# Four-layer token model on one core: semaphore clears in mid-stage, a key cache filled during the projection before attention, attention's first mask and values first

## The chip, the cores and the metric

The kernel runs on one core of a Trainium2 chip, as one launch. A core has five engines with a queue each: TensorE (PE, with PEld for its weight loads), VectorE (DVE), ScalarE (ACT), GpSimd (POOL) and SyncE (SP), which issues nearly all DMAs here. The metric is the device time of one execution in microseconds (us); before the change the median of three runs is 3574.46 us (3572.65 to 3577.14).

## The reference, cut to what matters

2048 tokens of width 512 pass through four layers, each a conditional product and a feed-forward part added to the tokens. The layer around the change is the third: attention with grouped heads over a paged cache of keys and values.

```
q = einsum(x, Wq)  [32 heads x 128];  k, v = einsum(x, Wk), einsum(x, Wv)  [8 heads x 128]
q, k = rope(rmsnorm(q)), rope(rmsnorm(k))
kc, vc = k_cache[block_table], v_cache[block_table]       # 16 pages of 32 tokens for each sequence
k_all, v_all = concat([kc, k]), concat([vc, v])           # 512 cached + 32 new tokens
scores = einsum(q, k_all) * SCALE;  scores where cached token >= cache_seqlens: -1e30
o = softmax(scores) @ v_all;   x = x + lora_mix(o @ Wo)
```

All of it is float32. Each product is made as three TensorE passes over a high and a low part of both operands: ScalarE copies the tile rounded (the high part, fp32r), and VectorE or GpSimd subtracts that from the tile (the low part).

## The kernel before, in words

The program is a row of stages, each one function and one block of code for the five engines: `l0_cond`, `l0_ffn`, `l1_up`, `l1_down`, `moe` (kind 1, which gives x2), `l2_qkv`, `l2_attn`, `l2_out`, `moe` (kind 2), `l3`. A stage takes its semaphores and on-chip memory when it begins and gives the memory back when it ends. All engines meet at the end of each block (a DRAIN of each queue, then an exchange of semaphores), so no engine starts the next stage before the slowest has ended this one. The order inside a queue is the order of the code; nothing plans it at run time.

Semaphores of a stage are cleared by SP in the stage after it, by `before.clear(sp)`, one instruction for each semaphore (line 54). In eight of the nine stages that have it this is SP's last work before the block ends; in `l3` it stands between the last store and the waits for the last eight stores to land.

In `l0_ffn` SP does for each of the 16 token tiles: fetch a later x tile, wait until VectorE has finished this tile (`done`), store it (line 500), load four numbers from a table and issue four small DMAs for `wg` (line 504).

`l2_qkv` keeps the tokens, turned (`xT`, 64 KB in each partition for both parts), and runs 8 head groups x 16 token tiles = 128 steps: 24 matmuls for q, k, v; ScalarE copies and squares (1722, 1725, 1729), VectorE sums and applies the cosine, GpSimd the sine and the root (1673, 1676), ScalarE scales (1695), PE turns the heads (1807), ScalarE and VectorE split them in parts (1702, 1706, 199), SP stores them (1626, 1629, 1649). Slots for the stored tiles are two deep: ScalarE waits until the store two steps back has landed. One DMA at the start of the eighth head group already fetches the first 16 pages of the key cache into `stage`.

`l2_attn` has 2 halves of heads x 64 sequences = 128 groups of 4 units. `Kall` holds the 64 pages of a half's key cache as high and low parts. It is made in four chunks of 16 pages: fetch into one of three stage buffers (1 MB), high part on ScalarE (line 2017), low part on VectorE or GpSimd (line 199). Then, for each group, VectorE and GpSimd copy the 16 pages that the sequence's table names from `Kall` into `K` (line 1901), two buffers deep. VectorE adds the new keys (2059) and makes the mask (2063). A unit is: scores on PE (line 194), add mask and take the maximum on VectorE (2092), exponential on ScalarE (2041), scaling on VectorE (2102, 2105), and five and six units later the turning of the probabilities (2156) and the product with the values (2170, 2171). GpSimd gathers the values (1997). Before its loop VectorE makes the row numbers of the values (2069), converts the lengths (2071), makes the low parts of chunks 0, 2 and 3, copies 10 pages of the first group and makes its mask; GpSimd makes the low part of chunk 1 and copies 6 pages. Chunks 4 to 7 belong to the second half of the heads.

Of the kernel before, what the change touches and what calls it, by code (L numbers as in the profile page):

```python
# [6 lines left out]
F32 = mybir.dt.float32  # L7
# [6 lines left out]
P = 128  # L14
NT = 16
# [7 lines left out]
class Stage:  # L23
# [22 lines left out]
    def slots(self, name, n, shape, dt=F32, each=1, sems=None):  # L46
        return Slots(self, name, n, shape, dt, each, sems)
# [9 lines left out]
class Slots:  # L57
# [3 lines left out]
    def __init__(self, st, name, n, shape, dt, each, sems):  # L61
        self.n, self.each = n, each
        self.bufs = [st.sb(f"{name}{i}", shape, dt) for i in range(n)]
        self.sems = sems or [st.sem(f"{name}{i}") for i in range(n)]
# [347 lines left out]
def l0_ffn(nc, A, S, before):  # L412
# [62 lines left out]
    with nc.Block() as block:  # L475
        @block.sync
        def _(sp):
# [28 lines left out]
            before.clear(sp)  # L506
# [170 lines left out]
def l1_up(nc, A, S, before):  # L677
# [62 lines left out]
    with nc.Block() as block:  # L740
        @block.sync
        def _(sp):
# [45 lines left out]
            before.clear(sp)  # L788
# [160 lines left out]
def l1_down(nc, A, S, before):  # L949
# [39 lines left out]
    with nc.Block() as block:  # L989
        @block.sync  # L990
        def _(sp):
# [45 lines left out]
            before.clear(sp)  # L1037
# [276 lines left out]
def moe(nc, A, S, before, kind, Beside):  # L1314
# [5 lines left out]
    base = st.pair("base", [P, 4, D])  # L1320
    gc = st.pair("gc", [P, 4, G + P])
    bt = st.pair("bt", [P, 1, D])
    dT = [st.pair(f"dT{i}", [P, 4, P]) for i in range(8)]
# [24 lines left out]
    with nc.Block() as block:  # L1348
        @block.sync
        def _(sp):  # L1350
# [34 lines left out]
            before.clear(sp)  # L1385
# [186 lines left out]
def l2_qkv(nc, A, S, before):  # L1572
    st = Stage(nc, "l2q")
    ident, _ = S["ident"]
    xT = st.pair("xT", [P, 4, 2048])
    wq = [st.pair(f"w{i}", [P, 4, 768]) for i in range(2)]
    w = Weights(st, 3, 768, [(*sl(wq[hg % 2], S_, slice(k, k + 1), S_), rows_of(A["wqkv"][hg], k, 1)) for hg in range(8) for k in range(4)])
    pa = [st.ps(f"pa{i}", [P, 1024]) for i in range(2)]
# [20 lines left out]
    N = len(steps)  # L1599
    begin, finish = {0: 0, 1: 1, 6: 2, 8: 3}, {5: 0, 7: 1, 10: 2, 12: 3}  # L1600
# [12 lines left out]
    with nc.Block() as block:  # L1613
        @block.sync
        def _(sp):
# [15 lines left out]

            for k in range(3):
                w.fetch(sp, k)
            for k in range(10, 16):
                sp.wait_ge(*before_x.landed(k))
# [5 lines left out]
            for n, (hg, tt) in enumerate(steps):  # L1641
                if n == 7 * NT:
                    sp.dma_start(st0[:, :, :], A["kT"][0, 0:16].rearrange("a p n -> p a n")).then_inc(st0_in, 16)
# [6 lines left out]
                if n >= 2:  # L1650
                    stores(n - 2)
            stores(N - 2)
            stores(N - 1)
            before.clear(sp)

        @block.gpsimd
        def _(pool):
            pool.memset(half[:, :], -0.5).then_inc(half_set, 1)
# [20 lines left out]
        def _(act):  # L1679
# [32 lines left out]
            for n, (hg, tt) in enumerate(steps):  # L1712
# [19 lines left out]
                if n >= 2:  # L1732
                    turned_parts(n - 2)
# [842 lines left out]
```

## Time and profile before

| | us |
|---|---|
| median of 3 runs | 3574.46 |
| the profiled execution | 3580.38 |
| its span, first to last instruction | 3578.6 |
| busy PE, DVE, ACT, POOL | 3332.9, 2323.6, 1762.9, 1386.7 |

A group of instructions is named by line, engine, operation, output and inputs. "Idle before" is time in which the engine stood still just before the instruction, with what ended the wait. The stages end, in us from the span's start, at 96.7, 405.6, 784.6, 965.1, 1083.8, 1724.3, 3020.9, 3383.4 and 3489.1, and the last at 3578.6.

### The profile page before, as it was taken

How to read it: one execution, taken by the hardware profiler on the slowest of the kernel's cores; microseconds unless marked ns; L12 is line 12 of the kernel's file. 1: busy time of each engine (PE TensorE's matmuls, PEld its weight loads, DVE VectorE, ACT ScalarE, POOL GpSimd, SP SyncE). 2: the span in 40 equal slices, each digit the busy share in tenths (PEclk: the TensorE clock that was granted, in tenths of full speed). 3: DMA queues.
4: the chain of work that ended last, by engine and by line, in shares of the span. 5: the costliest groups of instructions: out<-in, count | busy, mean ns of one | idle time of the engine just before them, and what ended most of it. 6: DMA issues, size and time to landing. Idle time of an engine off the chain costs nothing. (4 is left out here: it accounts for less than half of the span.)

```text
span 3578.6 us, 69531 instructions
## 1 busy us (share of the span) xinstructions
PE 3332.9 (93%) x22314; PEld 3076.0 (86%) x22314; DVE 2323.6 (65%) x6558; ACT 1762.9 (49%) x4289; POOL 1386.7 (39%) x2439
## 2 busy tenths in 40 slices
PE   7899699989788999999499999989999998999888
PEld 5688699988677888888499999989999998888677
DVE  5444343334286877777688988878888886422274
ACT  3322122223225777887466666656666665322222
POOL 0221100000035777887455655645565563100022
PEclk9899799999889999999799999999999999999999
DMA  5310442324335555555666666656666665533333
GB/s 202 127 55 25 96 110 81 81 90 146 92 114 162 168 175 178 172 180 164 202 210 212 220 209 211 221 171 212 220 209 212 219 211 188 180 109 109 109 115 121
DMA packets 444290, 562.49 MB, mean 157 GB/s; under 512 B 170712, under 2 KB 330264, under 8 KB 427033
## 3 DMA queue, kind: packets, MB, share of 16 engines
q1 hardware_dynamic: 424216, 419.63, 37.9%
q0 software_dynamic: 19712, 138.42, 11.2%
q8 instruction: 180, 2.95, 0.3%
q14 instruction: 182, 1.48, 0.1%
HBM read 389.36 MB, written 168.56 MB: 156 GB/s over the span
## 5 line engine op out<-in xcount | busy, mean ns | idle before, releaser
L1901 POOL CAST l2a_K<-l2a_Kall 128x256 fp32r x1524 | 597.4, 442 | 428.1 <-issue 422.2
L194 PE MATMUL l2a_s<-l2a_K,l2a_Q 128*128 128x288 f32 (+1 forms) x3072 | 521.1, 306 | 49.0 <-DVE l2a_K L2059 38.6
L2170 PE MATMUL l2a_x<-l2a_pt,l2a_V 128*128 128x128 f32 x4096 | 543.0, 276 | 4.9 <-DVE l2a_pn L2111 4.9
L2170 PEld LDWEIGHTS l2a_x<-l2a_pt,l2a_V 128*128 128x128 f32 x4096 | 503.9, 193 | 5.4 <-issue 5.2
L194 PEld LDWEIGHTS l2a_s<-l2a_K,l2a_Q 128*128 128x128 f32 x3072 | 428.3, 192 | 50.2 <-issue 49.3
L2092 DVE CUSTOM_DVE_ANT_0 l2a_sm<-l2a_s,l2a_B 128x544 f32<-128x544 f32 x512 | 369.3, 721 | 92.0 <-PE l2a_s L194 80.1
L2041 ACT ACTIVATE l2a_p<-l2a_sm,l2a_st 128x544 f32<-128x544 f32 x512 | 379.6, 741 | 31.1 <-DVE l2a_st L2095 29.8
L2027 ACT ACTIVATE l2a_pt<-l2a_t 128x512 f32<-128x512 f32 x512 | 305.6, 597 | 127.8 <-PE l2a_t L2156 127.1
L142 POOL TENSOR_TENSOR moe_btL<-moe_stage,moe_btH 128x512 fp32r<-128x512 f32 x2 | 5.7, 2850 | 881.5 <-ACT moe_btH L137 881.5
L2156 PE MATMUL l2a_t<-ident,l2a_p 128*128 128x128 f32 x2048 | 335.4, 286 | 5.9 <-ACT l2a_ao L2034 5.9
L2156 PEld LDWEIGHTS l2a_t<-ident,l2a_p 128*128 128x128 f32 x2048 | 287.9, 209 | 7.2 <-issue 6.6
L2102 DVE TENSOR_SCALAR l2a_p<-l2a_p,l2a_st 128x512 f32<-128x512 f32 x512 | 281.6, 550 | 18.2
L2034 ACT ACTIVATE l2a_ao<-l2a_x 128x128 f32<-128x128 f32 x512 | 142.2, 278 | 281.8 <-PE l2a_x L2171 281.8
L1673 POOL TENSOR_TENSOR l2q_rot<-l2q_qs,sinq 128x256 f32<-128x256 f32 x256 | 192.1, 772 | 137.2 <-ACT l2q_qs L1722 137.2
L1695 ACT ACTIVATE l2q_qn<-l2q_qn,l2q_r 128x128 f32<-128x128 f32 x640 | 200.3, 396 | 0.8 <-DVE l2q_qn L1778 0.8
L2171 PE MATMUL l2a_x<-l2a_pn,l2a_vn 128*128 128x128 f32 x1024 | 198.5, 276 | 0.0
L1676 POOL TENSOR_TENSOR l2q_r<-l2q_r,l2q_eps 128x5 f32<-128x5 f32 x128 | 193.4, 1511 | 0.0
L1769 DVE TENSOR_REDUCE l2q_r<-l2q_sq 128x5 f32<-128x640 f32 x128 | 105.2, 822 | 117.1 <-ACT l2q_sq L1729 117.0
L194 PE MATMUL l2q_pa<-l2q_w0H,l2q_xTH 128*128 128x512 f32 (+1 forms) x512 | 178.8, 349 | 0.0
L194 PE MATMUL l2q_pa<-l2q_w1H,l2q_xTH 128*128 128x512 f32 (+1 forms) x512 | 178.1, 348 | 0.0
L194 PE MATMUL l2q_pa<-l2q_w0H,l2q_xTL 128*128 128x512 f32 (+1 forms) x512 | 173.6, 339 | 0.0
L194 PE MATMUL l2q_pa<-l2q_w1H,l2q_xTL 128*128 128x512 f32 (+1 forms) x512 | 172.9, 338 | 0.0
(812 smaller groups left out, 8856.1 us busy)
## 6 DMA issues: line engine op xcount, KB each, us to landing
s_qT<-l2q_qo SPq DMA_DIRECT2D x128, 512.0 KB, 3.0
l2a_Q<-s_qT SPq DMA_DIRECT2D x128, 512.0 KB, 5.9
s_ao<-l2a_ao SPq DMA_DIRECT2D x64, 512.0 KB, 5.0
l2o_a<-s_ao SPq DMA_DIRECT2D x128, 256.0 KB, 3.1
s_kn<-l2q_ko SPq DMA_DIRECT2D x128, 128.0 KB, 3.1
l2a_kn<-s_kn SPq DMA_DIRECT2D x32, 512.0 KB, 5.8
l2q_stage<-in_wqkv SPq DMA_DIRECT2D x32, 384.0 KB, 4.1
s_act<-l1u_ac SPq DMA_DIRECT2D x88, 128.0 KB, 1.9
```

The costliest lines, as they stand in the source:

```text
L194: i = pe.matmul(out, a, b, start=start and m + z == 0, stop=stop and 3 * m + z == n - 1)
L1673: pool.tensor_tensor(r[:, hs, a], q[:, hs, z], sn[:, tt, a].unsqueeze(1).broadcast_to([P, hs.stop - hs.start, 64]), ALU.mult).then_inc(tur ...
L1676: pool.tensor_tensor(f[:, 10:15], f[:, 5:10], half[:, :], ALU.pow).then_inc(rooted, 1)
L1695: act.activation(o[:, h, :], o[:, h, :], ACT.Copy, scale=f[:, 10 + h:11 + h]).then_inc(scaled, 1)
L1901: e.tensor_copy(K[:, j:j + 1, :, :].rearrange("p a z n -> p a (z n)"), Kall[:, bass.ds(v, 1), :, :].rearrange("p a z n -> p a (z n)")).the ...
L2027: act.activation(ptr[tr % 2][:, :, :], ps_t[tr % 2][:, :, :], ACT.Copy).then_inc(t_copied, 1)
L2041: act.activation(prr[sc % 6][:, :], smr[sc % 2][:, :], ACT.Exp, bias=s[:, 1:2], scale=SCALE, accum_out=s[:, 2:3]).then_inc(exped, 1)
L2092: dve.tensor_tensor_reduce(out=smr[sc % 2][:, :], in0=ps_s[sc % 2][:, 224:768], in1=Br[g % 2][:, :], scale=1.0, scalar=-3e38, op0=ALU.add, ...
L2102: dve.tensor_scalar(p[:, 0:512], p[:, 0:512], s[:, 3:4], None, ALU.mult).then_inc(scaled, 1)
L2156: m = pe.transpose(ps_t[tr % 2][:, k, :], p[:, k:512:4], ident[:, :])
L2170: pe.matmul(px[:, P:256], V[:, k * D + hg * P:k * D + hg * P + P], pt[:, k, :], start=k == 0, stop=False)
L2171: pe.matmul(px[:, P:256], vn[:, hg, :], pnr[g % 2][:, :], start=False, stop=True).then_inc(pv_mm, 1)
```

## The change

1. `before.clear(sp)` moves from the end of the stage into its middle: after the middle tile (`l0_ffn`, both `moe`), after the fourth of eight column groups (`l1_up`), after the third of four (`l1_down`), after half the head groups, units or steps (`l2_qkv`, `l2_attn`, `l2_out`), and after tile 11 of 16 in `l3`. In `l0_ffn` the table load and the four `wg` DMAs of a tile go ahead of the wait for `done` and the store.
2. Memory for the key cache (`cache`, 64 KB in each partition), the first group's keys (`keys`) and `head` is taken before `moe` kind 1. The tiles of `moe` kind 1 lie in `cache`, and then `xT` of `l2_qkv` does, one slice for each token tile. The weights of the even head groups lie in `keys` and `head`.
3. In the sixth head group of `l2_qkv` SP fetches, one in each step, the 16 pages of the first sequence by its table. In the eighth, each step has one more high part (ScalarE) and low part (VectorE) of four pages: steps 0 to 3 make the first sequence's keys straight into `keys`, steps 4 to 15 make cache pages 0 to 47 in the places of the token tiles that are no longer needed. SP also fetches the first group's q and new keys, and leaves pages 48 to 63 fetched but not split. GpSimd waits at the start of `l2_qkv` for the last stores of x2.
4. `l2_attn` starts with that. VectorE: new keys, lengths, mask of group 0, then the row numbers of the values; chunk 3's low part comes after the first unit's maximum. GpSimd gathers the first group's values first and then copies 12 pages for the second. Chunks 4, 5 and 6 are fetched in units 4, 8 and 12.

```diff
@@ l0_ffn, SP
                 x_tile(tt + 2)
-                sp.wait_ge(done, tt + 1)
-                sp.dma_start(S["x1"][tt * P:(tt + 1) * P, :], xr[tt][:, :]).then_inc(xr.sem(tt), 16)
                 sp.reg_load(r, subj[0:1, 4 * tt:4 * tt + 4])
                 for j in range(4):
...
+                sp.wait_ge(done, tt + 1)
+                sp.dma_start(S["x1"][tt * P:(tt + 1) * P, :], xr[tt][:, :]).then_inc(xr.sem(tt), 16)
+                if tt == NT // 2:
+                    before.clear(sp)
-            before.clear(sp)
@@ l2_qkv, SP
+            def cache_pages(i):
+                sp.wait_ge(part_lo, i - 3)
+                sp.dma_start(st0[:, 4 * (i % 4):4 * (i % 4) + 4, :],
+                             A["kT"][0, 4 * (i - 4):4 * (i - 3)].rearrange("a p n -> p a n")).then_inc(st0_in[i % 4], 16)
...
+                if hg == 5:
+                    page(tt)
+                if hg == 7 and tt >= 1:
+                    cache_pages(tt + 3)
+                if n == 7 * NT + 1:
...
+                    sp.dma_start(q0..., S["qT"][0, 0]).then_inc(q0_in, 16)
+                    sp.dma_start(kn0..., S["kn"][0, 0]).then_inc(kn0_in, 16)
+                if n == 4 * NT:
+                    before.clear(sp)
             stores(N - 2)
+            cache_pages(19)
             stores(N - 1)
-            before.clear(sp)
@@ l2_qkv, ScalarE and VectorE, at the end of a step
+                if hg == 7:
+                    act.wait_ge(*key_part_in(tt))
...
+                    act.activation(key_part(tt, 0), st0[:, 4 * (tt % 4):4 * (tt % 4) + 4, :], ACT.Copy).then_inc(part_hi, 1)
+                if hg == 7:
+                    dve.wait_ge(part_hi, tt + 1)
+                    low_part(dve, [key_part(tt, z) for z in range(2)], st0[:, 4 * (tt % 4):4 * (tt % 4) + 4, :]).then_inc(part_lo, 1)
@@ l2_attn, GpSimd
             pool.wait_ge(rows_set, 2)
+            values(0)
             pool.wait_ge(tab_in, 16)
-            low(1)
-            for n in range(4):
-                chunk_done(pool, n)
-            page_copies(pool, r, 0, range(10, 16), pages_g)
+            chunk_done(pool, 3)
@@ l2_attn, ScalarE
-            for n in range(4):
-                high(n)
+            high(3)
@@ l2_attn, VectorE
-            for n in (0, 2, 3):
-                low(n)
-            for n in range(4):
-                chunk_done(dve, n)
-            page_copies(dve, r, 0, range(5), pages_v)
-            page_copies(dve, r, 0, range(5, 10), pages_v)
+            new_keys(0)
...
             mask(0)
...
+                    if sc == 0:
+                        low(3)
+                        chunk_done(dve, 3)
+                        dve.wait_ge(tab_in, 16)
```

## Rows read from the trace of the kernel before

**Rows 1.** The page: busy time, share of the span, instructions of an engine.

```profile
PE 3332.9 (93%) x22314; PEld 3076.0 (86%) x22314; DVE 2323.6 (65%) x6558; ACT 1762.9 (49%) x4289; POOL 1386.7 (39%) x2439
```

**Rows 2.** Busy time by stretch: us, engines, granted clock, DMA share, GB/s.

```profile
1640.00:1715.00 75.00, 72.51 (x446) 64.77 (x445) 56.79 (x113) 57.62 (x160) 56.51 (x81) 1.00 0.52 169
1724.30:1757.30 33.00, 0.00 (x0) 0.00 (x0) 12.82 (x18) 7.64 (x4) 8.83 (x12) 0.50 0.73 208
```

**Rows 3.** Line 54 by stretch, six of nine: ns min/median/max, first to last start.

```profile
L54 SPq EVENT_SEMAPHORE_RANGE_CLEAR  x39: 25/25/49, 402.8 to 405.4; - x39
L54 SPq EVENT_SEMAPHORE_RANGE_CLEAR  x41: 25/25/29, 782.2 to 784.4; - x41
L54 SPq EVENT_SEMAPHORE_RANGE_CLEAR  x30: 25/25/25, 1082.0 to 1083.6; - x30
L54 SPq EVENT_SEMAPHORE_RANGE_CLEAR  x43: 25/25/34, 1721.7 to 1724.1; - x43
L54 SPq EVENT_SEMAPHORE_RANGE_CLEAR  x23: 25/25/40, 3487.2 to 3488.8; - x23
L54 SPq EVENT_SEMAPHORE_RANGE_CLEAR  x36: 25/25/25, 3576.0 to 3577.9; - x36
```

**Rows 4.** Timeline of SP around the end of l0_ffn: start, us, instruction.

```profile
400.06 0.35 SPq L500 DMA_DIRECT2D s_x<-l0f_xr  x1
400.91 1.83 SPq L504 DMA_DIRECT2D wg<-in_w  x4
```

**Rows 5.** Line 475, l0_ffn's block end: GpSimd's drain, in ns.

```profile
L475 POOLq DRAIN  x1: 2693/2693/2693, 398.0 to 398.0; - x1
```

**Rows 6.** Lines 1034 and 2218, the stores of d, and their time to landing.

```profile
L1034 SPq DMA_DIRECT2D s_d<-l1d_o x16: 319/320/532, 844.9 to 962.2; - x16
DMA to landing us min/median/max: 2.3/2.4/3.6
L2218 SPq DMA_DIRECT2D s_d<-l2o_o x16: 319/320/338, 3118.2 to 3380.8; - x16
DMA to landing us min/median/max: 2.4/2.8/4.5
```

**Rows 7.** Timeline of SP: first loads that read the stage before.

```profile
966.18 0.93 SPq L1355 DMA_DIRECT2D moe_dr<-s_d  x2
...
3022.50 1.29 SPq L2203 DMA_DIRECT2D l2o_a<-s_ao  x3
...
3384.72 0.93 SPq L1355 DMA_DIRECT2D moe_dr<-s_d  x2
```

**Rows 8.** Timeline of the start of attention.

```profile
1726.97 0.41 DVE L2069 TENSOR_SCALAR l2a_rows<-l2a_tabx,l2a_pr 128x64 int32<-128x64 int32 x2 [6.03 <-DMA l2a_pr<-in_p]
...
1734.50 4.51 POOL L199 TENSOR_TENSOR l2a_Kall<-l2a_stage,l2a_Kall 128x2048 fp32r<-128x2048 f32 x1 [9.15 <-ACT l2a_Kall L2017]
...
1736.90 2.15 DVE L2071 CAST l2a_seq<-l2a_seqi 128x64 f32<-128x64 int32 x1 [9.52 <-DMA l2a_seqi<-in_seq]
...
1749.74 2.29 DVE L199 TENSOR_TENSOR l2a_Kall<-stage,l2a_Kall 128x2048 fp32r<-128x2048 f32 x1 [6.29 <-ACT l2a_Kall L2017]
...
1753.96 6.82 POOL L1901 CAST l2a_K<-l2a_Kall 128x256 fp32r x18 [14.96 <-issue]
...
1757.35 5.62 PE L194 MATMUL l2a_s<-l2a_K,l2a_Q 128*128 128x288 f32 x24 [38.58 <-DVE l2a_K L2059]
...
1759.09 0.72 DVE L2092 CUSTOM_DVE_ANT_0 l2a_sm<-l2a_s,l2a_B 128x544 f32<-128x544 f32 x1 [1.33 <-PE l2a_s L194]
...
1767.51 0.71 DVE L2092 CUSTOM_DVE_ANT_0 l2a_sm<-l2a_s,l2a_B 128x544 f32<-128x544 f32 x1
```

**Rows 9.** Timeline of one steady step of l2_qkv.

```profile
1645.11 0.71 ACT L1722 ACTIVATE l2q_qs<-l2q_pa 128x640 f32<-128x640 f32 x1 [1.14 <-PE l2q_pa L194]
...
1645.89 1.45 POOL L1673 TENSOR_TENSOR l2q_rot<-l2q_qs,sinq 128x256 f32<-128x256 f32 x2 [1.17 <-ACT l2q_qs L1722]
...
1646.64 0.82 DVE L1769 TENSOR_REDUCE l2q_r<-l2q_sq 128x5 f32<-128x640 f32 x1 [1.08 <-ACT l2q_sq L1729]
```

More of the change, by code:

```diff
@@ L1036, in _ @@
                     fetch(cb + 2, range(FT))
-            before.clear(sp)
+                if cb == 2:
+                    before.clear(sp)
         @block.scalar
@@ L1319, in moe, with pair @@
     ident, _ = S["ident"]
[L1320 to L1323, printed above, removed]
+    pair = st.pair
+    if kind == 1:
+        room = S["cache"][:, :, :, :].rearrange("p a z n -> p (a z n)")
+        taken = [0]
+        def pair(name, shape):
+            n = int(np.prod(shape[1:]))
+            at, taken[0] = taken[0], taken[0] + 2 * n
+            return tuple(room[:, at + z * n:at + z * n + n].rearrange("p (a n) -> p a n", a=shape[1]) for z in range(2))
+    base = pair("base", [P, 4, D])
+    gc = pair("gc", [P, 4, G + P])
+    bt = pair("bt", [P, 1, D])
+    dT = [pair(f"dT{i}", [P, 4, P]) for i in range(8)]
     dr = st.slots("dr", 6, [P, 4, P])
@@ L1651, in _ @@
                     stores(n - 2)
+                if n == 4 * NT:
+                    before.clear(sp)
             stores(N - 2)
+            cache_pages(19)
             stores(N - 1)
-            before.clear(sp)
         @block.gpsimd
         def _(pool):
+            for k in range(10, 16):
+                pool.wait_ge(*before_x.landed(k))
             pool.memset(half[:, :], -0.5).then_inc(half_set, 1)
@@ L1829, in l2_qkv @@
     before.marks.close()
-    S["qkv_stores"] = [(r, N - 2 + i) for r in (qo, ko, vs) for i in range(2)]
+    S["qkv_stores"] = qo, ko, vs
     return st
@@ L1841, in l2_attn @@
     st0, st0_in = S["stage"]
-    stage = [(st0, st0_in)] + [st.const(f"stage{i}", [P, 16, P]) for i in range(2)]
-    Kall = st.sb("Kall", [P, NB, 2, P], F32R)
+    stage = [(st0, st.sem("stage0"))] + [st.const(f"stage{i}", [P, 16, P]) for i in (1, 2)]
+    Kall, K0, (q0, q0_in), (kn0, kn0_in) = S["cache"], S["keys"], S["q0"], S["kn0"]
     tab, tab_in = st.const("tab", [1, NB * 16], I32)
@@ L2080, in _ @@
             mask(0)
+            dve.wait_ge(tabx_in, 16)
+            dve.wait_ge(pr_in, 16)
+            for h in range(2):
+                dve.tensor_scalar(rows[:, h, :], tabx[:, :], 8.0, pr[:, h:h + 1], ALU.mult, ALU.add).then_inc(rows_set, 1)
             for i in range(U + LV):
@@ L2491, in build @@
         stage = ExitStack()
-        S["stage"] = stage.enter_context(nc.sbuf_tensor("stage", [P, 16, P], F32)), outer.enter_context(nc.semaphore("s_stage"))
+        S["stage"] = (stage.enter_context(nc.sbuf_tensor("stage", [P, 16, P], F32)),
+                      [outer.enter_context(nc.semaphore(f"s_stage{i}")) for i in range(4)])
+        S["cache"] = stage.enter_context(nc.sbuf_tensor("cache", [P, NB, 2, P], F32R))
+        S["keys"] = stage.enter_context(nc.sbuf_tensor("keys", [P, 17, 2, P], F32R))
+        S["head"] = stage.enter_context(nc.sbuf_tensor("head", [P, 3072], F32R))
+        for i, n in enumerate(("q0", "kn0")):
+            S[n] = (S["head"][:, 1024 * i:1024 * i + 1024].rearrange("p (h z x) -> p h z x", h=4, z=2),
+                    outer.enter_context(nc.semaphore(f"s_{n}")))
         with ExitStack() as mid:
```

141 lines of the change are left out of this document (86 added, 55 removed).

## The prediction

> **What bounds the kernel now.** I read the engines' busy time first: PE is busy 93% of the span and the others far less [rows 1]. So time goes either with PE's own work, which this change leaves alone, or with the stretches where PE stands. The table by stretch shows both: in the projection (`l2_qkv`) PE is busy 72.5 of 75 us at the full granted clock, while for the 33 us at the start of attention it has no matmul at all [rows 2]. That gap is the largest target. The timeline of its start says what is late: VectorE and GpSimd split four chunks of the key cache and copy the first group's pages, and PE's first scores at 1757.35 end 38.58 us of idleness [rows 8]. The rows of line 54 show the second target: at the end of each stage SP clears 23 to 43 semaphores one after the other, while every other engine stands at the block's end [rows 3]. Six of the nine runs stand there; the three others (ends of `l1_down`, `l2_attn`, `l2_out`) look alike.
>
> **Part 1, the clears.** What counts is when the block would end without them, and whether the next stage then finds its data. In mid-stage they cost nothing, I say: SP has waits in each stage, and its next issues come a few us ahead of need. If that cover were gone, each run of clears would cost at most its own 1.6 to 2.6 us once.
>
> - `l0_ffn`: the last x1 store is issued at 400.06 + 0.35; after it come 4 `wg` DMAs (1.83) and the clears up to 405.4 [rows 3, 4]. With the DMAs ahead of the wait, both go. GpSimd's drain ends at 398.0 + 2.7 = 400.7, and that becomes the last [rows 5]. 405.4 - 400.7 = 4.7 us.
> - `l1_up`: 782.2 to 784.4 and the last one's own time: 2.3 us [rows 3]. The next stage begins with weights and tiles stored long before.
> - First `moe` to `l2_qkv`: 1082.0 to 1083.6 is 1.7 us [rows 3]. The first weights are fetched that much earlier. One more small DMA (the table) stands before the token loads, 0.3 us at the issue; the weights' chain is the longer, so I keep 1.7. GpSimd's new wait for x2 holds up a memset and one low part whose weight has not landed yet: nothing.
> - `l2_qkv` to `l2_attn`: 1721.7 to 1724.1, 2.4 us [rows 3].
> - Second `moe` to `l3`: 3487.2 to 3488.8, 1.7 us [rows 3]; `l3` begins with weights.
> - `l1_down` to `moe`: here the next stage must read what was just stored. The last store starts at 962.2 and lands 2.4 later at the median, so at 964.6 [rows 6]; the first load of d could be issued at about 964.8 instead of 966.18 [rows 7]. 1.4 us, between 0.4 (its longest landing, 3.6) and 2.3 (the clears whole).
> - `l2_out` to `moe`: 3380.8 + 2.8 = 3383.6 [rows 6] against 3384.72 [rows 7]: 1.0 us, between 0 and 2.1.
> - `l2_attn` to `l2_out`: the first load of the attention output goes at 3022.50 [rows 7], nearly 2 us into the stage, and before it stand only one weight fetch and the wait for the last store. It will go then again. Only the weights are ahead of it: 0.4 us, between 0 and 1.4.
> - End of `l3`: the last clear starts at 3577.9 [rows 3] and stands beside the landing of the last store, which takes 2 us like the others in [rows 6]: 0.3 us, between 0 and 0.5.
>
> Sum: 4.7 + 2.3 + 1.7 + 2.4 + 1.7 + 1.4 + 1.0 + 0.4 + 0.3 = 15.9 us.
>
> **Part 2, the start of attention.** I compare the moment of unit 4's maximum, the first of the second group, from which both kernels run alike. It is 1767.51 now, 8.4 us after unit 0's at 1759.09 [rows 8]. With the clears gone the stage starts at about 1722.0 (1721.7 and the exchange at the block's end) [rows 3]. Then:
>
> - Data for the mask: nothing large is queued ahead now. Of DMAs in attention's first microseconds, the row numbers' inputs were there at 1726.97, 2.6 us into the stage [rows 8]; the new order puts the lengths and `iota` (272 KB) first, behind the last stores and the last 256 KB of key pages. I take 3.5 us: 1725.5. Bounds: 2.6, and 8 us (the lengths came 12.6 us after the stage's start with 3 MB around them, at 1736.90 [rows 8], so I take under that).
> - VectorE: new keys are done by then; conversion 0.2, mask 0.7 (as wide as the 0.72 of a maximum), row numbers 0.41. Unit 0's maximum at 1726.8. PE has its scores long before.
> - After it VectorE has one thing more than now, chunk 3's low part, 2.29 [rows 8]. ScalarE's high part (no longer than that, begun with the stage or when the last pages land) is ready. Unit 4 at 1726.8 + 8.4 + 2.3 + 0.1 = 1737.6.
> - GpSimd must not be later: low part done at 1730.1, then 12 page copies at 6.82 / 18 = 0.38 each [rows 8], 4.6 us: 1734.7. Unit 4's scores are due at about 1736. It fits with 1.3 us.
>
> Gain 1767.5 - 1737.6 = 29.9 us, of which 2.4 is the clears' already: 27.5 us here. Bounds 21 and 29.5.
>
> A row shows a conversion of 128x64 taking 2.15 us on VectorE (1736.90) while GpSimd's low part runs from 1734.50 for 4.51; both end at 1739.0 [rows 8]. I price it at 0.2 because in the new order GpSimd has only its memsets (about 1 us) then. The Trainium skill (SBUF — State Buffer, section "SBUF: two separate sides") says that VectorE and GpSimd share a pair of ports under an exclusive lock which the loser waits for during the whole instruction. The row agrees. By this rule the same lock speaks against part 3: the added low part there has two inputs on chip.
>
> **Part 3, what the eighth head group now carries.** 16 steps each get a high part of 128x512 on ScalarE and a low part on VectorE, 0.6 us (0.71 for 128x640 [rows 9]) and 0.7 us (a quarter of the chunk's 2.29 [rows 8] and a fixed part). A step takes about 4.7 us (446 matmuls, 29 a step, in 72.5 us [rows 2]), and both engines have room in it: ScalarE waits 1.14 us for PE, VectorE 1.08 for ScalarE [rows 9]. The low part comes right before that wait, so 0.4 us of room is left on each. On SP each step gains one DMA, 0.7 us at most, behind a wait for the low part of the step before; queued behind it is the store of v and then those of q and k, whose slots ScalarE needs two steps or 9.4 us later; with some 3 us to land (2.4 to 2.8 for such stores [rows 6]) and 2 us to fill and split, I estimate 4 us to spare. DMA traffic rises from 169 GB/s at a share of 0.52 [rows 2] by 256 KB per step, 55 GB/s, to a share of about 0.69. Nothing shows on PE: 0 us, between 0 and 10 (0.6 us a step, the whole high part, if the room is not where I see it). Pages and first group's q: single DMAs beside the same steps, nothing. If the rule of the shared ports holds, GpSimd begins its products (1645.89 [rows 9]) up to 0.35 us late in each step; it stands idle 1.17 us before them, so the rule would cost nothing until VectorE's part moves by 0.8 us, and then at most 0.35 x 16 = 5.6 us, which lies inside those bounds.
>
> **Part 4, small debts.** Chunks 4, 5 and 6 were fetched while PE stood and now fall on units 4, 8 and 12, 1 MB each beside q and values: 0.5 us, between 0 and 5. PE's granted clock was 0.50 over the 33 us [rows 2]; the new start has sparse scores for 15 us, so PE may still be at 1.2 GHz when the work gets dense: 1 us, between -1 and 4. `xT` and the tiles of `moe` kind 1 in other memory: the same shapes and runs, 0.
>
> **The sum.** 15.9 + 27.5 - 0.5 - 1.0 = 41.9 us. Against the profiled execution: 3580.38 - 41.9 = 3538.5. The median is 5.9 us lower than that execution: 3574.46 - 41.9 = 3532.5.
>
> **Rivals.**
>
> - *The projection pays.* For: the room on ScalarE and VectorE is only about 1.1 us, and the new work takes 0.6 to 0.7 of each and ties SP, ScalarE and VectorE in one more ring. Against: PE fills the step and waits for none of them. Price: 1 us a step, 16 us: 3548.5. Chance 0.08.
> - *The first unit waits for its DMAs.* Lengths and `iota` land 8 us into the stage instead of 3.5, behind the last stores: 4.5 us less, 3537. For: they were very late before. Against: those 3 MB are no longer there. Chance 0.12, together with a later chunk 3.
> - *Only the clears pay.* The second group's keys become what all waits for: chunk 3's fetch must land in full, go through ScalarE and VectorE, and then through 12 copies on GpSimd, and this chain replaces the old one. Price, were the start of attention to save nothing beyond the waits at its ends: 3574.5 - 15.9 = 3558.6. Against: three of four chunks are split before. Chance 0.02.
> - *Slower.* The place is the eighth head group's stores: SP's wait for the low part delays the stores of q and k, their slots come free late, ScalarE stops, the low part gets later still. It decides at 41.9 / 16 = 2.6 us a step, 7.3 instead of 4.7; at 3.2 us a step the time is 3574.5 + 9.5 = 3584. Against: it needs stores some 4 us later than they are. Chance 0.03.
> - *The moves do less harm than I price*, and loads after a block's end find their data at once: 3528. Chance 0.05.
>
> **How the numbers follow.** 0.70 is left for the forecast, with its own range 3528 to 3537. For 8 in 10 the range reaches up over the DMA rival and into the projection's and down over the last: 3525 to 3544. About 0.2% (7 us) is what a measurement of this kernel tells from no change: above 3567 only the slower rival and slips that I did not see: faster 0.95, same 0.02, slower 0.03.
>
> **What would show it.** Line 54 in the middle of each stage and SP's first issue of a stage within 0.3 us of its last one before, 4.7 us earlier against `l0_ffn`'s last store. PE's first scores within 1 us of the start of attention; unit 0's maximum 5 us and unit 4's 15.6 us after it. Steps of the eighth head group still 4.7 us apart, with ScalarE's and VectorE's waits shrunk to about half a microsecond. I am wrong if those steps grow, if unit 4 waits for GpSimd's copies, or if a long wait for values appears in the first four groups.

## The result, and the profile after

The changed kernel takes 3534.98 us at the median of four runs (3528.07 to 3536.73); the kernel before, with them, 3575.8 (3572.65 to 3579.39). The ratio, estimated from all runs, is 0.9882 (95% interval 0.9865 to 0.9899), and the medians differ by 40.8 us where 41.9 were forecast. A second series (kernel 4 below) gave 3533.99 against 3575.59, 0.9881 (0.9866 to 0.9896), 41.6 us.

The two profiled executions differ by more, 3580.38 - 3528.07 = 52.3 us, because this one of the changed kernel was its fastest and that of the kernel before was slower than all four of its timed runs. The stages' lengths, read between the ends of their blocks, show where (us; mean granted clock in brackets where it moved):

| stage | before | after | difference |
|---|---|---|---|
| `l0_ffn` | 308.9 (0.89) | 295.3 (0.92) | -13.6 |
| `l1_up` | 379.0 | 373.7 | -5.3 |
| `l1_down` | 180.5 | 176.6 | -3.9 |
| first `moe` | 118.7 | 115.8 | -2.9 |
| `l2_qkv` | 640.5 | 639.5 | -1.0 |
| `l2_attn` | 1296.6 | 1270.4 | -26.2 |
| `l2_out` | 362.5 | 362.3 | -0.2 |
| second `moe` | 105.7 | 104.0 | -1.7 |
| `l3` | 89.4 (0.92) | 92.0 (0.89) | +2.6 |

Busy time on the page, against [rows 1]: every engine has nearly the same work as before, so what went is mostly idle time, and in `l0_ffn` some of PE's busy time, by its clock.

```profile
PE 3330.7 (94%) x22314; PEld 3073.8 (87%) x22314; DVE 2323.7 (66%) x6562; ACT 1767.3 (50%) x4302; POOL 1384.0 (39%) x2432
```

The table by stretch of the changed kernel (us, then the busy time of PE, PE's weight loads, VectorE, ScalarE and GpSimd with instructions, granted clock, DMA share, GB/s): `l0_ffn`, the eighth head group, and the start of attention up to the second group's first scores. The last two answer to [rows 2].

```profile
96.70:391.80 295.10, 272.38 (x1264) 228.08 (x1264) 127.53 (x232) 76.41 (x124) 73.93 (x69) 0.92 0.20 65
...
1610.00:1686.00 76.00, 76.00 (x467) 67.84 (x466) 67.19 (x127) 65.48 (x175) 61.18 (x81) 1.00 0.69 214
1697.40:1714.40 17.00, 6.59 (x25) 5.77 (x25) 10.52 (x28) 4.45 (x7) 7.59 (x16) 0.50 0.64 199
```

The eighth head group carries the new parts at the full clock, with PE busy in all of its 76 us and at the DMA share of 0.69 that was forecast. The 33 us without a matmul have become 17 with 25 of them. `l0_ffn` before had 281.63 us of PE at a clock of 0.89: 9.25 us of the 13.6 are the same 1264 matmuls run at a higher granted clock.

Line 54 of the changed kernel, three of nine stages, against [rows 3]: the same counts, in mid-stage, 12 us (`l3`) and more before its end.

```profile
L54 SPq EVENT_SEMAPHORE_RANGE_CLEAR  x39: 25/25/34, 307.0 to 309.1; - x39
```
```profile
L54 SPq EVENT_SEMAPHORE_RANGE_CLEAR  x43: 25/25/31, 1393.5 to 1396.2; - x43
```
```profile
L54 SPq EVENT_SEMAPHORE_RANGE_CLEAR  x36: 25/25/40, 3511.4 to 3513.7; - x36
```

SP's timeline around the end of `l0_ffn` (start, us, instruction), against [rows 4], and GpSimd's drain against [rows 5]:

```profile
391.06 0.35 SPq L506 DMA_DIRECT2D s_x<-l0f_xr  x1
391.94 0.35 SPq L159 DMA_DIRECT2D l1u_nat<-s_x  x1
```
```profile
L476 POOLq DRAIN  x1: 2693/2693/2693, 389.0 to 389.0; - x1
```

From the start of the last store to that of the next stage's first issue it is 0.88 us now. The drain ends at 389.0 + 2.69 = 391.7, the stage at 391.8.

SP's stores of d and the first loads of it (ns min/median/max, first to last start; then start and us), against [rows 6, 7]:

```profile
L1037 SPq DMA_DIRECT2D s_d<-l1d_o x16: 319/320/516, 824.5 to 941.5; - x16
```
```profile
L2292 SPq DMA_DIRECT2D s_d<-l2o_o x16: 319/320/333, 3067.0 to 3329.6; - x16
```
```profile
944.24 0.93 SPq L1369 DMA_DIRECT2D moe_dr<-s_d  x2
...
2971.32 0.81 SPq L2277 DMA_DIRECT2D l2o_a<-s_ao  x2
...
3332.78 0.38 SPq L1369 DMA_DIRECT2D moe_dr<-s_d  x1
```

The timeline of the start of attention, against [rows 8]; the stage begins at 1697.5:

```profile
1697.59 0.35 SPq L2013 DMA_DIRECT2D l2a_iota<-in_iota  x1
1697.98 1.05 SPq L2014 DMA_DIRECT2D l2a_seqi<-in_seq  x1
1698.41 3.06 PE L195 MATMUL l2a_s<-keys,head 128*128 128x288 f32 x12 [4.18 <-DVE keys L2130]
1703.51 0.20 DVE L2143 CAST l2a_seq<-l2a_seqi 128x64 f32<-128x64 int32 x1 [5.24 <-DMA l2a_seqi<-in_seq]
1703.81 0.50 DVE L2139 TENSOR_SCALAR l2a_B<-l2a_iota,l2a_seq 128x544 f32<-128x544 f32 x1
1704.55 0.72 DVE L2162 CUSTOM_DVE_ANT_0 l2a_sm<-l2a_s,l2a_B 128x544 f32<-128x544 f32 x1
1705.38 2.28 DVE L200 TENSOR_TENSOR cache<-stage,cache 128x2048 fp32r<-128x2048 f32 x1
1708.99 5.13 POOL L1971 CAST l2a_K<-cache 128x256 fp32r x12 [3.02 <-issue]
1714.32 3.06 PE L195 MATMUL l2a_s<-l2a_K,l2a_Q 128*128 128x288 f32 x12 [3.01 <-POOL l2a_K L1971]
1716.06 0.72 DVE L2162 CUSTOM_DVE_ANT_0 l2a_sm<-l2a_s,l2a_B 128x544 f32<-128x544 f32 x1 [0.34 <-PE l2a_s L195]
```

PE's first scores come 0.9 us into the stage instead of 33. VectorE then waits for the lengths until 1703.51, 6.0 us in. Unit 0's maximum is at 7.0 and unit 4's at 18.6; before they were at 34.8 and 43.2. PE's second group waits 3.01 us, for GpSimd's copies.

The last step of the eighth head group, against [rows 9]:

```profile
1686.52 0.70 ACT L1782 ACTIVATE l2q_qs<-l2q_pa 128x640 f32<-128x640 f32 x1 [0.62 <-PE l2q_pa L195]
1686.98 0.68 DVE L200 TENSOR_TENSOR cache<-stage,cache 128x512 fp32r<-128x512 f32 x1
1687.31 1.63 POOL L1733 TENSOR_TENSOR l2q_rot<-l2q_qs,sinq 128x256 f32<-128x256 f32 x2 [0.87 <-ACT l2q_qs L1782]
1688.05 0.82 DVE L1836 TENSOR_REDUCE l2q_r<-l2q_sq 128x5 f32<-128x640 f32 x1 [0.39 <-ACT l2q_sq L1789]
1690.00 0.63 ACT L1800 ACTIVATE cache<-stage 128x512 fp32r<-128x512 f32 x1
```

The parts cost 0.63 and 0.68 us; ScalarE's wait fell from 1.14 to 0.62, VectorE's from 1.08 to 0.39, GpSimd's from 1.17 to 0.87, and its two products took 1.63 instead of 1.45. Over the first 14 steps of that head group the mean waits of ScalarE and VectorE are 0.66 and 0.45 us, against 1.13 and 1.07 before.

One thing in `l2_qkv` did change outside this head group. VectorE's sum of squares runs once in each of the 128 steps; its row before and after (last two figures: first and last start):

```profile
L1769 DVE TENSOR_REDUCE l2q_r<-l2q_sq x128: 821/822/825, 1103.8 to 1712.9; 128x5 f32<-128x640 f32 x128
```
```profile
L1836 DVE TENSOR_REDUCE l2q_r<-l2q_sq x128: 821/822/824, 1077.6 to 1688.1; 128x5 f32<-128x640 f32 x128
```

The same 127 steps take 609.1 us before and 610.5 after. It is in every head group from the second on: its 16 steps take 75.76 us in each of the four profiles with the tiles in their old places (before, kernels 1, 2 and 9), and 75.95 or 76.05 in each of the ten with the new ones (kernel 6's eighth group aside). That is 0.19 or 0.29 us for each of seven head groups, 1.3 to 2.0 us in the stage. (The two profiles of the changed kernel itself, this one and kernel 4's, have 75.95 and 76.05.)

### The profile page after: what moved, and what is told of

Same layout as the page of the kernel before. It is cut to its first block and busy times, and to the rows that moved or that the text cites. A ratio compares the mean times of both kernels' runs of the same rounds, so it can differ in the third digit from the quotient of the medians.

```text
span 3526.3 us, 69602 instructions
## 1 busy us (share of the span) xinstructions
PE 3330.7 (94%) x22314; PEld 3073.8 (87%) x22314; DVE 2323.7 (66%) x6562; ACT 1767.3 (50%) x4302; POOL 1384.0 (39%) x2432
## 5 line engine op out<-in xcount | busy, mean ns | idle before, releaser
L1971 POOL CAST l2a_K<-cache 128x256 fp32r x768 | 295.3, 434 | 222.4 <-issue 222.4
L1971 POOL CAST keys<-cache 128x256 fp32r x750 | 299.2, 449 | 187.8 <-issue 149.9
L195 PE MATMUL l2a_s<-keys,head 128*128 128x288 f32 (+1 forms) x1536 | 262.2, 307 | 17.8 <-POOL l2a_K L1971 7.2
L195 PE MATMUL l2q_pa<-keys,cache 128*128 128x512 f32 (+1 forms) x1024 | 268.4, 344 | 0.0
L195 PE MATMUL l2q_pa<-l2q_w1H,cache 128*128 128x512 f32 (+1 forms) x1024 | 267.7, 344 | 0.0
L195 PE MATMUL l2a_s<-l2a_K,l2a_Q 128*128 128x288 f32 (+1 forms) x1536 | 261.0, 306 | 3.4 <-POOL l2a_K L1971 3.0
L195 PEld LDWEIGHTS l2a_s<-keys,head 128*128 128x128 f32 x1536 | 215.0, 193 | 18.9 <-issue 16.1
L195 PEld LDWEIGHTS l2a_s<-l2a_K,l2a_Q 128*128 128x128 f32 x1536 | 214.5, 192 | 3.9 <-issue 3.3
L195 PEld LDWEIGHTS l2q_pa<-keys,cache 128*128 128x128 f32 x1024 | 180.9, 190 | 21.7
L195 PEld LDWEIGHTS l2q_pa<-l2q_w1H,cache 128*128 128x128 f32 x1024 | 180.2, 189 | 21.6
```

The source lines that it names most:

```text
L195: i = pe.matmul(out, a, b, start=start and m + z == 0, stop=stop and 3 * m + z == n - 1)
L1971: e.tensor_copy(K[:, j:j + 1, :, :].rearrange("p a z n -> p a (z n)"), Kall[:, bass.ds(v, 1), :, :].rearrange("p a z n -> p a (z n)")).the ...
```

## The experiments

Each is compared with runs of the kernel before on the same chip. Kernels 1 to 4 shared a chip, 5 to 8 another, 9 to 12 a third, with 12 in a series of its own; across series the ratios are compared, and 0.001 is 3.6 us. A gain is the difference of two medians and can lie 1 to 1.5 us from what the ratio gives. Lengths of stages are those of one profiled execution.

### 1 to 4. The two halves apart

1: the kernel before with the clears in mid-stage. 2: this, and `l0_ffn`'s DMAs ahead of the wait. 3: the changed kernel with the clears at the ends and the old order in `l0_ffn`. 4: the changed kernel again.

```diff
@@ 1, from the kernel before: the form for l0_ffn and moe; in the other stages the condition names their own middle
+                if tt == NT // 2:
+                    before.clear(sp)
-            before.clear(sp)
```

> The kernel before with only the semaphore clears moved to mid-stage; the order of the wg DMAs in l0_ffn and all of the key cache as before. My theory: each stage end loses its run of clears where the next stage does not wait for a landing: 13.8 us less than before (15.9 of the prediction less 2.1 for the wg DMAs), 12 to 16. Rival (the changed kernel's profile shows l0_ffn 13.8 us shorter and l1_up 5.3, so the clears in mid-stage did more than vanish from the end): 22 us or more. Rival (mid-stage clears hold up SP's DMAs and cost elsewhere): under 8 us.

> As e1_clears, and in l0_ffn the table load and the four wg DMAs of a tile ahead of the wait for done and the store. My theory: 15.9 us less than before, 2.1 less than e1_clears. Rival (the order of these DMAs, not the clears, makes l0_ffn 13.8 us shorter): 8 us or more less than e1_clears.

> The changed kernel with the clears back at the end of each stage and the old order in l0_ffn: the key cache, first mask and values alone. My theory: 26 us less than before (27.5 less 1.5 of small debts); the changed kernel's profile has unit 4's maximum 18.5 us into attention against 43.2, so 24.7 us if the projection pays nothing. Rival (the eighth head group pays 1 us a step): 9 us. With e2_clears_order it should add up to the whole: 41.

> The changed kernel again, beside the others on one chip: 41 us less than before (39 to 44), the sum of e2_clears_order and e3_keys_only within 2 us. Rival (the parts share a gain, or one spoils another): the sum is off by over 3 us. If the 52 us between the two profiled executions are the change's and not a matter of the granted clock in l0_ffn, its stage is shorter than 297 us in this profile too and its granted clock 0.92 against 0.89.

| | median | before | ratio (95%) | gain |
|---|---|---|---|---|
| 1 clears | 3562.83 | 3575.59 | 0.9967 (0.9953-0.998) | 12.8 |
| 2 clears and order | 3555.97 | 3575.59 | 0.9949 (0.9936-0.9963) | 19.6 |
| 3 the rest alone | 3553.01 | 3575.59 | 0.9934 (0.9921-0.9948) | 22.6 |
| 4 all | 3533.99 | 3575.59 | 0.9881 (0.9866-0.9896) | 41.6 |

The halves add up: 19.6 + 22.6 = 42.2 against 41.6. Both pay, in the sizes forecast within some 4 us: 15.9 for kernel 2's part, and 27.5 - 0.5 - 1.0 = 26.0 for kernel 3's; both figures lie inside the intervals. That the clears alone pay (3558.6) is thereby refuted as the whole story: it is half of it. Kernel 2 is 6.9 us below kernel 1 where 2.1 were expected, nearer to its rival (8 or more, from the order of `l0_ffn`'s DMAs); kernel 9 tests that. In kernel 4's profile `l0_ffn` took 298.6 us at a granted clock of 0.91, so the 295.3 at 0.92 above is not the changed kernel's steady figure.

### 5. The mask's inputs fetched in `l2_qkv`

```diff
@@ l2_qkv, SP, n == 7 * NT + 1; these tiles now lie in the two token buffers
+    for n_, src_ in (("iota", A["iota544"]), ("seqi", row_bc(A["seq"], NB)),
+                     ("tabx", A["tabx"]), ("pr", A["p8"])):
+        sp.dma_start(S["e_" + n_][0], src_).then_inc(S["e_" + n_][1], 16)
@@ l2_attn, SP: these four DMAs go; VectorE, after new_keys(0):
+            for r_ in S["qkv_stores"]:
+                for k_ in range(8 * NT - 2, 8 * NT):
+                    dve.wait_ge(*r_.landed(k_))
```

> The changed kernel with iota, lengths and the inputs of the row numbers fetched in the eighth head group of the projection (into the two token buffers, free by then) instead of at the start of attention; VectorE waits for the projection's last stores before the mask, since its tiles lie where these stores read. In the changed kernel the first unit's maximum stands at 7.0 us into attention, after a wait for the lengths that ends at 6.0. My theory (DMA landing after the block's end is the term I undersized, 6.0 us against 3.5): unit 0 at 3.5 to 4.5 us, unit 4 at 15 to 16 instead of 18.5, 3 us less than the changed kernel. Rival (GpSimd's 12 page copies for the second group set unit 4): the first units come early, unit 4 moves by under 1 us, same time.

3530.17 us against 3576.13, 0.9874 (0.9857 to 0.9892): 46.0 us. In attention the step is clear: 1266.8 us against 1270.4 in the changed kernel and 1270.2 in kernel 4. Its start, at 1703.2, on the timeline:

```profile
1704.05 3.06 PE L195 MATMUL l2a_s<-keys,head 128*128 128x288 f32 x12 [4.21 <-DVE keys L2128]
...
1706.24 0.20 DVE L2144 CAST l2a_seq<-nat 128x64 f32<-128x64 int32 x1 [2.34 <-DMA s_kn<-l2q_ko]
...
1707.29 0.72 DVE L2163 CUSTOM_DVE_ANT_0 l2a_sm<-l2a_s,l2a_B 128x544 f32<-128x544 f32 x1
...
1711.72 5.10 POOL L1973 CAST l2a_K<-cache 128x256 fp32r x12 [3.02 <-issue]
...
1717.04 3.06 PE L195 MATMUL l2a_s<-l2a_K,l2a_Q 128*128 128x288 f32 x12 [2.99 <-POOL l2a_K L1973]
```

Unit 0's maximum is 4.1 us into the stage instead of 7.0, unit 4's 15.6 instead of 18.6. The wait that is left, 2.34 us, is for the last stores. Attention took 1269.7 to 1270.4 us in the five other profiles whose clears and chunks stand as in the changed kernel (4, 6, 8, 10, 12), so 3.5 us is well outside what this stage varies by. So the lengths' DMA held the whole start, and all that follows moved by what it lost. The total, 0.0007 under kernel 4's ratio, goes the same way but does not show it by itself. PE's wait for GpSimd's copies stayed at 3 us: that chain begins with chunk 3's low part, behind the first maximum.

### 6. The parts of the eighth head group twice

ScalarE makes each high part a second time and VectorE each low part.

```diff
+                    act.wait_ge(part_hi, 2 * tt + 1)
+                    act.activation(key_part(tt, 0), st0[...], ACT.Copy).then_inc(part_hi, 1)
...
+                    dve.wait_ge(part_lo, 2 * tt + 1)
+                    low_part(dve, [key_part(tt, z) for z in range(2)], st0[...]).then_inc(part_lo, 1)
```

> The changed kernel with the high and the low part of each of the 16 steps of the eighth head group made twice (the same values). This uses up the room that the prediction claims: 0.6 us more on ScalarE and 0.7 us more on VectorE in each step, of some 0.6 and 0.4 left. My theory: PE's steps grow, but by no more than what goes over the room, 0.2 to 0.5 us a step, 3 to 8 us in all. Rival (the two engines are as good as full now, each part is paid whole): 10 us or more. Other rival (PE never waits for them at all, two steps of slack): under 1 us.

3544.81 against 3576.13, 0.9906 (0.9889 to 0.9922), so 0.0025 or 9 us above kernel 4's ratio; `l2_qkv` took 648.5 us against 639.5 and 640.2. A stretch of that head group, and three instructions from its timeline:

```profile
1632.00:1708.00 76.00, 70.85 (x427) 61.75 (x425) 74.51 (x131) 70.51 (x178) 63.83 (x73) 1.00 0.64 200
```
```profile
1660.57 1.58 ACT L1755 ACTIVATE l2q_qn<-l2q_qn,l2q_r 128x128 f32<-128x128 f32 x5 [0.45 <-DVE l2q_qn L1847]
...
1661.23 1.94 DVE L200 TENSOR_TENSOR cache<-stage,cache 128x512 fp32r<-128x512 f32 x2
1661.86 1.50 POOL L1733 TENSOR_TENSOR l2q_rot<-l2q_qs,sink 128x64 f32<-128x64 f32 x2
```

VectorE is busy 74.51 of 76 us and ScalarE now waits for it, not for PE; a step takes 5.25 us (from VectorE's pair at 1655.98 to the next at 1661.23) instead of 4.75. So the room that hid the change's parts was there and was nearly used up: of a second pair of parts, 8 to 9 us came through, at or just over the top of the 3 to 8 expected and under the 10 of the rival. VectorE is the engine that would have become the bound.

### 7. Chunks 4, 5 and 6 at the front

The first three fetches of 1 MB go ahead of the units again, as before the change, with the second group's q ahead of them.

```diff
+            fetch(1)
+            for n in (4, 5, 6):
+                start_chunk(n)
             for i in range(U + LV):
...
-                    if sc in (4, 8, 12):
-                        start_chunk(sc // 4 + 3)
```

> The changed kernel with key chunks 4, 5 and 6 (1 MB each) fetched right at the start of attention, after the second group's q, as the kernel before did, instead of in units 4, 8 and 12. My theory: in units 4 to 12 they cost almost nothing (0.5 us), so at the front they can only cost: 0 to 5 us more, where the first values land later. Rival (they disturb values and q in the first groups): 2 us or more less.

3536.62, 0.9881 (0.9861 to 0.9901): no difference in total. Attention took 1272.7 us, 2.3 to 2.5 more than with them moved. Its timeline shows the bill, 23 us into the stage (which began at 1707.7):

```profile
1711.82 5.45 SPq L1991 DMA_DIRECT2D l2a_stage<-in_kT  x2
...
1722.88 5.06 SPq L2010 DMA_DIRECT2D l2a_vn<-s_vn  x4
...
1730.85 1.93 PE L2245 MATMUL l2a_x<-l2a_pt,l2a_V 128*128 128x128 f32 x8 [1.81 <-DMA l2a_vn<-s_vn]
...
1734.58 0.72 DVE L2163 CUSTOM_DVE_ANT_0 l2a_sm<-l2a_s,l2a_B 128x544 f32<-128x544 f32 x1 [2.07 <-PE l2a_s L195]
```

PE waits for new values queued behind the chunks, and unit 7's maximum waits 2.07 us for PE. Spreading the fetches saves these 2 us; in units 4, 8 and 12 they cost nothing I could find.

### 8, 10 and 12. Why `l3` got longer

`l3` took 92.0 us instead of 89.4. The difference is there after its first four steps, at a lower granted clock, though its own clears only come later. 8: the second `moe`'s clears at its end again. 10: `l3`'s. 12: both.

```diff
@@ 8 and 12, moe
-                if tt == NT // 2:
+                if tt == (NT // 2 if kind == 1 else NT - 1):
@@ 10 and 12, l3
-                if tt == NT - 5:
+                if tt == NT - 1:
```

> The changed kernel with the clears in the second moe put back to its end (after its last store); all other clears stay in mid-stage. In four profiles l3 lasts 89.4 and 89.8 us with the clears before it and 91.1 to 92.0 without, and TensorE's granted clock in it is 0.92 and 0.92 against 0.89 to 0.91. My theory: the 1.7 us won at this boundary is given back in l3 at the lower clock, so the time is the same within 0.7 us and l3 is back at 89.6. Rival (the prediction's term holds, l3's spread is chance): 1.7 us more than the changed kernel.

> The changed kernel with l3's clears put back after its last store; all others in mid-stage. l3 lasts 90.9 to 93.1 us in the eight profiles with the clears after tile 11, and 89.4 and 89.8 in the two without; but the 2 to 3 us are there at the first tile already, before any clear. Theory: chance of TensorE's clock, the clears' place does nothing: the same time as the changed kernel within 1 us, l3 at 91 to 93. Rival (the place of the clears in l3 costs 2 us): l3 at 89.6 and 2 us less than the changed kernel.

> The changed kernel with two of its nine clears back at the end of their stages, those of the second moe and of l3 (everything else as in the changed kernel). Open is why l3 takes 91.1 to 93.1 us in every kernel whose clears were moved, with a granted clock of 0.66 early in it, and 89.0 to 89.8 in the three whose clears stand at the end. Theory A: it hangs on the instant at which l3 begins relative to the end of moe's work, and needs both clears in their old places: l3 again 89 to 90 us, moe 105 to 106, total within 2 us of the changed kernel's 0.988. Theory B: it comes from further up (the parts moved in earlier stages shift the clock's rhythm): l3 stays at 91 to 93 and the total is 0 to 3 us longer than the changed kernel's.

| | total, ratio (95%) | second `moe` | `l3` |
|---|---|---|---|
| after | 3534.98, 0.9882 | 104.0 | 92.0 |
| 8 | 3532.48, 0.9886 (0.9866-0.9905) | 104.0 | 91.6 |
| 10 | 3535.06, 0.9894 (0.9879-0.9909) | 103.7 | 93.0 |
| 12 | 3539.78, 0.9902 (0.9883-0.9921) | 107.0 | 89.6 |

The stretch from 20.9 to 30.9 us into `l3`, in the changed kernel, in kernel 12 and before (columns as above):

```profile
3455.00:3465.00 10.00, 8.72 (x32) 7.24 (x33) 3.40 (x7) 1.79 (x4) 2.55 (x2) 0.66 0.01 2
```
```profile
3471.10:3481.10 10.00, 9.30 (x52) 8.07 (x53) 3.96 (x8) 1.96 (x5) 3.85 (x3) 1.00 0.17 54
```
```profile
3510.00:3520.00 10.00, 9.12 (x52) 7.89 (x53) 4.02 (x7) 1.96 (x5) 3.86 (x3) 1.00 0.17 54
```

With both in their old places `l3` is short again, and with either one alone it isn't. Over all profiled executions: 89.0 to 89.8 in the four kernels with both at the end (before, 3, 9, 12), 90.9 to 93.1 in the other ten. In these ten the granted clock, back at 1.00 after the stage's first microseconds, falls to 0.50 once more between 20 and 30 us into `l3`; in the four it does not. The two stages together give 192.8 to 196.6 in the first four and 194.3 to 198.6 in the others. So what the clears win at these two ends, the lower granted clock in `l3` gives back. My theory for kernel 8, that the second `moe`'s end alone decides this, fell; kernel 10's, that it is chance and the clears' place does nothing, gave the 91 to 93 us that came, but kernel 12 and the split of all 14 profiles speak against it. Why a shift of 2 us sets the clock so is open, and kernel 12's total is 5 us from what the theory of the two ends expected, inside the overlap of the intervals.

### 9. `l0_ffn`'s order alone

```diff
@@ l0_ffn, SP, in the kernel before; its clears stay at the end
-                sp.wait_ge(done, tt + 1)
-                sp.dma_start(S["x1"]...)
                 sp.reg_load(r, subj[0:1, 4 * tt:4 * tt + 4])
...
+                sp.wait_ge(done, tt + 1)
+                sp.dma_start(S["x1"]...)
```

> The kernel before with only l0_ffn's table load and wg DMAs ahead of the wait for done; all clears at their ends. The step in the prediction was 2.1 to 2.4 us (4 DMAs of 1.83 and the load no longer behind the last store); e2_clears_order came out 6.9 us under e1_clears. My theory: 2.3 us is the real size and the rest of the 6.9 is TensorE's clock, so 2 to 4 us less than before. Rival (with these DMAs early, l0_ffn's inside runs 4 to 5 us faster as well: its first tile was done at 73.0 and 73.5 us with this order, 75.8 and 78.8 without): 6 to 8 us less than before, first tile done before 74.

3572.91 (12 runs) against 3571.56 (17), 1.0002 (0.9992 to 1.0012): nothing, and a gain over 2.9 us is outside the interval. The end of the stage did get shorter, 3.26 us from the last store to the next issue instead of 5.60, but the total does not show it, so both the 2 to 4 us expected and the rival's 6 to 8 missed. The order does not pay the 6.9 us between kernels 1 and 2 by itself. They are not plain noise between runs either: each of kernel 2's five runs (3555.41 to 3560.04) lies below each of kernel 1's six (3561.26 and more). Whether they come from the two moves together or from chance between two built kernels is open.

The same holds for the 13.6 us of `l0_ffn` in the table above. Over the profiled executions the stage took 308.9 and 307.1 us with neither move (before, 3), 303.2 and 302.9 with one (1, 9), and 293.6 to 302.4, 297.9 in the mean, in the ten with both. The step of 10 us between the first and the last is twice the 4.7 that the stage's end explains; the other 5 have no cause shown. One execution says little here: in the eleven kernels with the new order, which do the same work up to there, the first tile was done 72.5 to 78.0 us into the stage.

### 11. Kernels 5 and 10 together

> e5_early_mask with l3's clears back after its last store, as the fastest version to be had from these edits. Theory: as e5_early_mask, 3.5 us less than the changed kernel, unit 4's maximum 15.6 us into attention. Rival (l3's clears cost 2 us where they stand): 5.5 us less.

3532.79 against 3571.56, 0.9892 (0.9878 to 0.9906), and 2.3 us below kernel 10 in the same series; 3.5 below the changed kernel were expected. Attention took 1266.5 us and units 0 and 4 came at 4.0 and 15.5, as in kernel 5; `l3` 92.1. The mask's gain is there in both. In the total it is below what the intervals tell apart: kernel 5 has the lowest ratio of all, and whether it beats the changed kernel is shown by the stage, not by the sum.

## Why the prediction was right, point by point

**The sum** was right: 41.9 us forecast, 40.8 and 41.6 measured. Its two halves were off in opposite ways, the clears with the order 15.9 against 19.6 (the clears alone 13.8 against 12.8), the rest 26.0 against 22.6. That they cancel to within 1.1 us is partly luck: the terms that can be read in rows, below, come to 34 or 35 us (14.5 at the ends of the stages and 24.6 at the start of attention, less 1.3 to 2.0 and 0.4 in `l2_qkv` and 2 to 3 in `l3`), and about 5 us more lie inside `l0_ffn`, where the prediction has no term and no run shows a cause.

**The clears.** Read on SP from the start of the last store to the next stage's first issue (in the three rows from `l1_down` on, to the first load of what was stored), before and after:

| end of | before | after | saved | forecast |
|---|---|---|---|---|
| `l0_ffn` | 5.60 | 0.88 | 4.72 | 4.7 |
| `l1_up` | 2.87 | 0.72 | 2.15 | 2.3 |
| first `moe` | 2.26 | 0.73 | 1.53 | 1.7 |
| `l2_qkv` | 3.18 | 0.93 | 2.25 | 2.4 |
| second `moe` | 2.32 | 0.73 | 1.59 | 1.7 |
| `l1_down` | 3.93 | 2.69 | 1.24 | 1.4 |
| `l2_out` | 3.88 | 3.21 | 0.67 | 1.0 |
| `l2_attn` | 4.01 | 4.19 | -0.18 | 0.4 |
| `l3`, to the span's end | 3.02 | 2.50 | 0.52 | 0.3 |

That is 14.5 us against 15.9. Each was read from the row that would be last without the clears (GpSimd's drain, a store's landing), and that is why the three kinds came out apart, as forecast. The sign "within 0.3 us of its last one" was a little tight: from the end of the last issue to the next start it is 0.40 to 0.53 us. What the forecast missed is `l3`'s clock, +2 to 3 us. In mid-stage the clears cost nothing visible; a cost of a few us in a stage like `l1_up`, which took 373.7 to 380.6 us over the profiles, would not be seen.

**The start of attention** is the largest mis-sized term. Unit 4's maximum came at 1716.06 - 1697.5 = 18.6 us and not at 15.6, so the start saved 24.6 us beyond the clears instead of 27.5 (in the six other profiles with this start and the clears in mid-stage, 17.8 to 18.5). The failed step is "I take 3.5 us" for the mask's data: 6.0 us. Unit 0 came 2.2 us late by it (7.0 against 4.8). The other 0.7 us lie between unit 0 and unit 4, 11.5 us instead of 8.4 + 2.3 + 0.1 = 10.8, and there it is GpSimd: 12 copies at 5.13 / 12 = 0.43 us instead of 0.38, and begun at 1708.99, 1.3 us after chunk 3's low part was done at 1707.66, so that the "1.3 us" by which it was to fit became a wait of PE. That is one of the prediction's own signs of being wrong, "if unit 4 waits for GpSimd's copies", and it came, with 3.01 us of waiting and 0.7 us of time. Kernel 5 shows the first: with the data early, units 0 and 4 come at 4.1 and 15.6. That the latter is the forecast figure is chance: unit 0 is earlier than the 4.8 forecast and the way from it to unit 4 still 11.5. The rival "the first unit waits for its DMAs" was the direction in which it missed, halfway to its 8 us.

Why it took 6.0 us, kernel 3 shows in part. There the clears still stand between the last stores and the stage's start, at 1720.1:

```profile
1720.64 0.43 SPq L2009 DMA_DIRECT2D l2a_seqi<-in_seq  x1
...
1723.96 0.20 DVE L2137 CAST l2a_seq<-l2a_seqi 128x64 f32<-128x64 int32 x1 [3.05 <-DMA l2a_seqi<-in_seq]
```

The lengths are there 3.8 us into the stage, close to the 3.5 forecast, and SP issues them in 0.43 us. In the seven profiles with this start and the clears in mid-stage the issue takes 0.69 to 1.10 us and they land at 5.2 to 6.0. So the two parts of the change are not independent: with the clears gone the stage begins right behind the last stores, its first DMAs take longer, and of the 2.3 us won at the end of `l2_qkv` 0.4 to 1.2 come back in unit 4 (17.4 us in kernel 3, 17.8 to 18.6 in the seven). The prediction counted both in full.

The conversion of the lengths took 0.20 us beside an idle GpSimd, against 2.15 in [rows 8] beside GpSimd's low part, as forecast.

**The eighth head group** was right: 0 us on the steps (its 15 full steps take as long as those of the seventh, 71.20 us both), PE busy 76.00 of 76.00 us, DMA share 0.69. "0.4 us of room left" was 0.62 and 0.39. Kernel 6 shows that this room was what hid it: a second pair of parts costs 0.5 us a step, half the price of the rival "the projection pays". GpSimd's products grew while VectorE's low parts ran: 128x64 twice in 1.50 us in kernel 6, against 0.60 before. The Trainium skill (SBUF — State Buffer, section "SBUF: two separate sides") has VectorE and GpSimd exclude each other on shared ports, and the trace agrees; with one low part a step the stretching vanished in GpSimd's own wait, as forecast. At the stage's end one thing was overlooked: the last fetch of pages (0.96 us of SP at 1695.05) stands between the last stores. From the last step's transposes to the last store it was 1721.18 - 1711.21 = 9.97 us and is 1696.66 - 1686.33 = 10.33: 0.4 us.

**The tiles in other memory** are a term put at nothing, "the same shapes and runs, 0", and that failed: every head group from the second on takes 0.19 to 0.29 us longer, 1.3 to 2.0 us in all, in each of the ten profiles with the new places and in none of the four with the old. With the 0.4 us at the end it accounts for most of what `l2_qkv` grew by: 639.0 to 640.5 us with the keys made there (kernel 6 aside), 637.5 and 638.9 in kernels 1 and 2. The head groups whose weights do not lie in `keys` and `head` grew as much as the others, so these two are not the whole cause; which move it is, no run separates.

**The debts.** Chunks 4 to 6 in their units cost nothing visible; at the front they would cost 2 us (kernel 7). The 1 us for PE's clock was not measured by itself. Both debts would lie between unit 4's maximum and the end of attention: 1253.3 us before and 1253.1 in kernel 9 against 1253.4 in kernel 3 (clears at the end), and 1251.1 and 1250.0 in kernels 1 and 2 against 1251.8 in the changed kernel (clears in mid-stage). So together they cost 0.1 to 1.8 us where 1.5 were priced.

## What to carry to other kernels

Housekeeping at a block's end costs the time from the event that would otherwise be last (a drain, a store's landing) to its own end; read that event for each block, since the saving ranged here from nothing to 4.7 us for the same loop. Work moved from a gap into a full loop was free here as long as it fitted the idle time of the engines it used, and doubling the moved work showed how near that edge was. Once the gap was closed, the next thing late was a small input that nobody waited for before, and it landed later the closer the stage began behind the last stores: give such an input a place ahead of the stage. And give memory that moves a term of its own: compare the length of a loop whose instructions did not change.

## What the runs showed of the hardware that was not expected

- The granted clock in `l3` differed with the place of two runs of clears of about 2 us each: over the same 10 us 1.00 with both at their stages' ends, and 0.66 in the changed kernel (between the levels of 2.4 and 1.2 GHz), worth 2 to 3 us. Why is open.
- `l0_ffn`, with 1264 matmuls in every kernel, had PE busy for 271.7 to 281.6 us at a mean granted clock of 0.92 to 0.89. A single profiled execution misjudges such a stage by more than most terms of this sum.
- Sixteen steps of `l2_qkv` at the full granted clock take the same time to 0.01 us in six head groups of one execution, and 75.76 us in all four profiles with the tiles in their old places. So a difference of 0.2 us can be read there: it is 75.95 or 76.05 us with the new places.
- SP's issue of one and the same small DMA, the lengths to all partitions, took 0.43 us in kernel 3 and 0.69 to 1.10 us where the stage began within 1 us of the last stores.
